# Top-64 attention on one NeuronCore: the copy of turned probabilities lags its item by one turn more

## What is computed

```python
scores = jnp.einsum('bhqd,bhkd->bhqk', qh, kh) / np.sqrt(DHEAD)
vals, idx = jax.lax.top_k(scores, topk)          # topk = 64 of 77 keys
scores = jnp.full_like(scores, neg).at[bI, hI, qI, idx].set(vals)
probs = jax.nn.softmax(scores, axis=-1)
ctx = jnp.einsum('bhqk,bhkd->bhqd', probs, vh)
return ctx.transpose(0, 2, 1, 3).reshape(...) @ wo_w.T + wo_b
```

## Time and profile before

| | us |
|---|---|
| median of 3 runs | 897.32 |
| lowest, highest | 896.64, 900.05 |
| the profiled execution | 897.16 |
| its span | 895.4 |
| PE busy | 801.0 (89%) |
| VectorE busy | 655.2 (73%) |
| ScalarE busy | 497.2 (56%) |
| GpSimd busy | 531.4 (59%) |
| mean granted TensorE clock | 0.968 |

### The profile page before, as it was taken

The page is one execution under the profiler, slowest core; times in us unless marked ns, Lnnn a source line. Parts: engine busy times, 40 slices in busy tenths (PEclk is TensorE's granted clock), DMA queues, the critical chain, the costliest instruction groups (busy, mean ns, idle before and its releaser), DMA issues.

```text
span 895.4 us, 18961 instructions
## 1 busy us (share of the span) xinstructions
PE 801.0 (89%) x5858; PEld 628.7 (70%) x5858; DVE 655.2 (73%) x2739; ACT 497.2 (56%) x1287; POOL 531.4 (59%) x721
## 2 busy tenths in 40 slices
PE   6999998998788676867887989999999999998897
PEld 5677775886566444645666779788778879987775
DVE  4888686888979999999999873455455542516887
ACT  5778764568997797978877331222112122226673
POOL 3565644676752978878775125456455545237883
PEclk9999999999999697979999899999999999999999
DMA  9200001000000082000222621222222243140011
GB/s 296 62 1 2 2 1 48 1 1 1 1 1 1 2 328 97 1 25 2 71 72 87 227 72 36 37 42 43 37 42 43 36 87 58 19 107 1 13 36 48
DMA packets 37823, 46.70 MB, mean 52 GB/s; under 512 B 4327, under 2 KB 33871, under 8 KB 37724
## 3 DMA queue, kind: packets, MB, share of 16 engines
q1 hardware_dynamic: 29243, 35.77, 11.9%
q0 software_dynamic: 8480, 9.72, 7.1%
HBM read 33.80 MB, written 11.68 MB: 51 GB/s over the span
## 4 chain that ended last, share of the span: by engine, by line
PE 64%; DVE 14%; ACT 8%; issue 6%; POOL 6%; another core or an unknown queue 1%; DMA 1%; DVEq 0%; ACTq 0%; POOLq 0%; SPq 0%
PE ps L3012 10%; PE ps L3023 10%; PE ps L2358 4%; PE ps L2454 3%; PE ps L2481 3%; PE ps L2780 3%; PE ps L2800 3%; PE ps L3067 2%; PE ps L3041 2%; PE ps L2439 2%; ACT ptall L1254 2%; PE ps L2466 2%; DVE experts L1812 1%; PE ps L2811 1%; PE ps L2866 1%
## 5 line engine op out<-in xcount | busy, mean ns | idle before, releaser
L2080 DVE COPY ptall<-experts 128x512 f32 x136 | 53.3, 434 | 97.8 <-PE ps L3012 49.1
L1388 ACT ACTIVATE wk<-ps 128x1024 f32<-128x1024 f32 x34 | 34.9, 1025 | 131.3 <-PE ps L3012 69.1
L3012 PE MATMUL ps<-xnT,ptall 128*128 128x128 f32 x896 | 105.0, 275 | 2.3 <-DVE ptall L2080 1.8
L3012 PEld LDWEIGHTS ps<-xnT,ptall 128*128 128x128 f32 x896 | 102.4, 192 | 3.0 <-issue 3.0
L3023 PE MATMUL ps<-experts,wk 128*128 x448 | 102.0, 381 | 1.4 <-ACT xkeep L1398 1.4
L3023 PEld LDWEIGHTS ps<-experts,wk 128*128 128x128 f32 x448 | 82.9, 190 | 17.0 <-issue 6.8
L848 POOL DMA_INDIRECT xn<-expert_in,rown x34 | 36.0, 1058 | 80.7 <-PE ps L2998 57.1
L646 POOL TENSOR_TENSOR experts<-experts,rden 128x616 f32<-128x616 f32 x32 | 38.9, 1217 | 46.8 <-DVE rden L1572 46.8
L872 POOL DMA_INDIRECT token_sum<-xkeep,dest x28 | 47.6, 1699 | 31.1 <-ACT xkeep L1398 22.5
L1229 ACT ACTIVATE experts<-experts 128x77 f32<-128x77 f32 x248 | 62.1, 258 | 0.0
L2358 PE MATMUL ps<-ones 128*128 128x256 bf16 x434 | 55.7, 286 | 5.8 <-POOL mone L599 5.8
(11 more groups left out here) (382 smaller groups left out, 2358.5 us busy)
## 6 DMA issues: line engine op xcount, KB each, us to landing
experts<-in_ew SPq DMA_DIRECT2D x16, 1024.0 KB, 8.5
xkeep<-in_bw SPq DMA_DIRECT2D x2, 1024.0 KB, 7.3
expert_in<-xkeep SPq DMA_DIRECT2D x8, 256.0 KB, 3.9
x<-token_sum SPq DMA_DIRECT2D x8, 256.0 KB, 3.8
out<-x SPq DMA_DIRECT2D x7, 256.0 KB, 2.2
x<-in_x SPq DMA_DIRECT2D x1, 1536.0 KB, 9.1
token_sum<-x SPq DMA_DIRECT2D x4, 256.0 KB, 2.6
token_sum<-x SPq DMA_DIRECT2D x1, 1024.0 KB, 4.5
```

The costliest lines, as they stand in the source:

```text
L2080: ins = nc.vector.tensor_copy(tilew[:, v, c, :], experts[:, bass.ds(e * EW + (c * FF + v * 512), 512)])
L3012: ins = nc.tensor.matmul(ps[j % 2][:, v, k * P:(k + 1) * P], tilew[:, v, c, k * P:(k + 1) * P], xTb[j % 3][:, c, :], start=c == 0, stop=c ...
```

## The change

On ScalarE the copy of turned probabilities of turn k is now that of item k-3 instead of k-2, and stands behind the absolute values and the scores and ahead of the exponentials; from turn 31 on it catches up (items 28 and 29 in one turn). The output copy moves from ahead of the scores to behind the exponentials. On PE the values of item k-3 stand at the head of turn k, behind the scores; the turning of x and the queries come one turn later (turns 4, 12, 20 and 5, 6, 13, 14, 21, 22) and ahead of the transposes of the same turn. The warming matmuls are left out where the turn has a part of the output projection. A wait for the copy of routing rows moves into top_values. No work is added.

```diff
@@ scalar, turn k @@
-                    if k >= 3 and (k - 3) // 2 % 2:
+                    if k >= N4 and (k - 3) // 2 % 2:
                         top_out(k - 3)
...
                     if 1 <= k < N4 - 1:
                         top_scores(k + 1)
+                    if 3 <= k < N4:
+                        top_turned_probs(k - 3)
                     if 1 <= k < N4:
                         top_exp(k - 1, 0)
...
+                    if 3 <= k < N4 and (k - 3) // 2 % 2:
+                        top_out(k - 3)
                     if k in top_parts:
                         top_residual(top_parts[k] // 4, top_parts[k] % 4, k)
-                    if 2 <= k < N4 + 2:
+                    if N4 - 1 <= k < N4 + 2:
                         top_turned_probs(k - 2)
@@ tensor, top_probs and top_values @@
-                    q, j = (i + 1) // ITEMS + 1, (i + 1) % ITEMS
+                    q, j = (i + 2) // ITEMS + 1, (i + 2) % ITEMS
                     pe.wait_ge(pt_s[4].sem, pt_s[4].past(i))
-                    if N4 - 9 <= i < N4 - 1:
+                    if N4 - 9 <= i < N4 - 1 and i + 2 not in top_parts:
                         warm(14, 4)
                     pe.wait_ge(nm_s, i + 1)
-                    if q < PAIRS and j == 3:
+                    if q < PAIRS and j == 4:
                         pe.wait_ge(xts[4].sem, xts[4].past(2 * q + 2))
-                    elif q < PAIRS and j in (4, 5):
-                        pe.wait_ge(q_s[4].sem, q_s[4].past(4 * q + 2 * (j - 3)))
+                    elif q < PAIRS and j in (5, 6):
+                        pe.wait_ge(q_s[4].sem, q_s[4].past(4 * q + 2 * (j - 4)))
...
+                    if i - 1 in l5_at:
+                        pe.wait_ge(xts[5].sem, xts[5].past(l5_at[i - 1] + 1))
@@ tensor, turn k @@
+                    if 3 <= k < N4:
+                        top_values(k - 3)
                     if k in top_parts:
                         top_final(top_parts[k] // 4, top_parts[k] % 4, k)
+                    if q + 1 < PAIRS:
+                        if j == 4:
+                            top_turn(q + 1)
+                        if j in (5, 6):
+                            top_queries(q + 1, j - 5)
                     if 2 <= k < N4 + 2:
                         top_probs(k - 2)
                         if k - 2 in l5_at:
                             l5_flip_half(l5_at[k - 2], k)
-                        if k - 3 in l5_at:
-                            pe.wait_ge(xts[5].sem, xts[5].past(l5_at[k - 3] + 1))
...
-                        top_values(k - 2)
+                        if k >= N4 - 1:
+                            top_values(k - 2)
...
-                    if q + 1 < PAIRS:
-                        if j == 3:
-                            top_turn(q + 1)
-                        if j in (4, 5):
-                            top_queries(q + 1, j - 4)
```

## The result

| | before | changed |
|---|---|---|
| median, us (20 runs of each) | 900.83 | 902.11 |
| lowest to highest | 895.31 to 903.31 | 899.15 to 909.43 |
| ratio, 95% interval | | 1.0036 (1.0019 to 1.0054) |
| span of the profiled execution | 895.4 | 900.1 |
| stretch from VectorE's first item to the start of the last values | 222.80 | 226.32 |

The changed kernel is slower by 0.36%, some 3.2 us (the means of the two differ by 3.0 us, the medians by 1.3). Forecast were 897.0 with a range of 893 to 902, and a kernel 0.4 us faster than before. The interval of the ratio leaves out 1, but the change is smaller than the 0.5% that the prediction's chances counted. The stretch runs from the first reduction of the top-64 items (at 273.67 and 275.71 us) to the start of the last values (496.47 and 502.03). It grew by 3.5 us, which is about the size of the whole loss.

The account below looks back on a forecast made before the run. VectorE was taken to bound the top-64 stage at 6.36 us an item, with 3.8 us of idle time to give back. From 897.16 us, -3.8 + 3.4 gave 896.8, stated as 897.0, range 893.0 to 902.0.

Parts of the forecast that it names:

- The old waits go: Top-64 stage: ScalarE's 20.2 us wait for turned probabilities goes, with VectorE's idle at items 12, 19, 20, 31; gain 3.8 us.
- Paces: ScalarE in the top-64 stage: its other work costs the same, a plain turn 4.2 us of 6.36.
- The new waits: Query copies, pairs 1 to 3: waits of 1.9 us, 3.3 in turns 14 and 22; 0.6 us idle at item 16.
- The clock, and pair 3: TensorE's half-clock windows stay; new VectorE idle 1.0, 1.2, 1.2 us in pairs 1 to 3, sum 3.4.
- Warming matmuls: Items 24 to 27 lose their 14 on TensorE; nothing comes back, range nothing to 2 us lost.
- The end: From turn 31 on the lag is caught up; taken as 0, with 0 to 1.1 us gained.
- clock falls in the query turns: Half clock in turns 12 to 14 or 20 to 22 lengthens waits: 904.8 us, last turn alone 900.6; chance 0.16.
- clean gain: ScalarE's query waits are hidden, new idle time 0, end gives 1.1 us: 892.3 us, 893.4 without the end; chance 0.15.
- No effect: VectorE's idle places come back because GpSimd's hold causes them, not the copy: 897.2 us; chance 0.05.
- GpSimd's hold: At turns 8 and 16 GpSimd stands for ScalarE's squares, 1.51 us; pair 3 starts 1.3 us late from it.

## Why the prediction was wrong

By its steps:

1. *The old waits go*: right in the main. The 20.2 us on flipped probabilities are gone, and so are the idle places at items 12 and 31. The 3.8 us were one execution's; a second had 3.0. Item 19 kept 0.18 us of 0.92, but item 20 did not go (0.87 for 0.65). Its turn 18, with the projection in a half-clock window, took 7.33 us; where the projection ran at full clock (the version with the warming matmuls back) it took 6.01 and item 20 had no idle time.
2. *Paces*: right in the main. Turns 13 and 14 came out within 0.03 us, though in turn 13 the query wait was shorter than worked out and ScalarE's other pieces 0.2 us longer, and turn 12 took 6.2 us for 6.4.
3. *The new waits*: right in number and place. Singly they are 1.66 and 3.00 us at full clock, not 1.9 and 3.3: the 0.3 us to drain was too much, for ScalarE's copy starts 0.03 us behind the last query matmul. That the sum is 14.2 again (14.4 in the second profile) is luck, as the wait of turn 21 at half clock makes up for it; with that turn at full clock it was 12.6. For pair 2 the 0.97 us at item 16 lie in the 0.6 to 1.2 that was summed, but the second profile had 1.66, and with turn 12 at half clock it was 2.8.
4. *The clock, and pair 3*: **this failed.** The sum gave pair 3 1.2 us; it took 4.0 (1.69 and 2.29), and 4.1 in the second profile. I kept the half-clock windows where the old order had them, while the lagged order has its own: in every profile of it but the one with the added matmuls a stretch of 6.8 us or more at half clock began between 411 and 421 us; in the five of the old order there was none there or one of 3.4. So turn 21, summed at full clock with 8.1 us, took 9.7, and turn 20, summed with 6.0, took 7.1; turn 22 was 8.7 as forecast. At full clock turn 21 took 8.13 us in the version with the added matmuls. The routing logits and flips ahead of its values, which the sum left out, cost nothing there; they count at half clock alone. The three turns took 25.6 us where 22.8 was summed, and the idle time is 2.8 us over the sum as well. Of these 2.8 the clock makes some 2.5 (1.6 in turn 21, and 0.9 in turn 20, an estimate from the added matmuls). The rest is the wait of the absolute values for the flips of turn 20, which the sum does not have. The range of pairs 2 and 3, 0.6 to 3 us each, did not reach it. Pair 1, given 1.0, took none and, in the second profile, some 0.6. The argument had also read the old clock too kindly: besides the three stretches it names, the kernel before has two of 3.4 us, from 358.2 (in turn 12) and from 443.6, so not all the query turns had run at 1.00.
5. *Warming matmuls*: their loss caused nothing that could be shown.
6. *The end*: no change beyond what two profiles of one kernel differ by (14.5 and 16.2 before, 15.6 and 14.8 after).

New idle time was 6.0 and 7.4 us instead of 3.4. Less the old 3.8 and 3.0, that is 2.2 and 4.4 us more; the end adds 1.0 in the first pair of profiles and gives back 1.3 in the second, and small gaps make up the 3.5 us by which the stretch grew in each. The rival *clock falls in the query turns* named the mechanism, and was given 0.16, because those turns had run at 1.00 in the old order. Its 900.6 is near what came, but by luck: it priced the last turn of a pair, at 3.9 us, and that turn (22) ran at full clock, while turns 20 and 21, priced at 1.5 and 2.6, ran partly at half. The rival *clean gain* is refuted by the six waits. *No effect* has the half of it that GpSimd's hold did cause the idle places of the old order at items 12 and 19. The absolute time was 5.1 us above the forecast, and 3.5 of that has another reason: the kernel before has a median of 900.8 over 20 runs, not the 897.3 of the three shown. Against the kernel before, the forecast was 0.4 us faster, and 3.2 us slower (by the ratio) came.

What stays open is what in the lagged order makes the clock fall in pair 3; the split between query waits and clock rests on the one profile with added matmuls. In the changed kernel TensorE's single waits for ScalarE's copy are longer (up to 4.2 us, 2.7 before; the lists of waits of TensorE from 289 to 480 us of the changed kernel and from 290 to 495 of the one before):

```profile
PE ps L2817 <- ACT ptall L1254: 35.3, 21, 4.2
```

```profile
PE ps L2811 <- ACT ptall L1254: 30.6, 26, 2.7
```

The longest do not stand ahead of the window at 417.4: there TensorE had stood 1.97 us ahead of the values of turn 20 and 0.83 us for the copy of turned x. With the added matmuls these were 1.38 and 0.83 us, and no window followed. Whether the shorter stand or the added work kept the clock up was not tested alone. The Trainium skill's page "TensorE: Matmul & The Clock Gate", section "HAM oscillation — how this bites in real kernels", describes a loop of short matmul bursts parted by waits for DMA, in which each burst starts cold again. The waits here are for ScalarE's copies, and the two profiles agree with it in kind.

## What to carry to other kernels

A lag that takes one wait out of a ring of two engines brings another in wherever a second user of the same buffer is squeezed into the same turn: write out the ring, turn by turn, for those turns alone, with everything TensorE does in them. Sum the granted clock as a result of the new order, not as a row of the old one, and let the range hold two more turns partly at half clock. Check a sum of waits one by one: here 14.2 us agreed while none of the six did. Where two profiles of one kernel differ by 2 us, an idle place of 1 us is a lead and not a finding.

## What the runs showed of the hardware

Fewer matmuls made the stretch no shorter: with half of the query matmuls it was 227.7 us (226.3 and 227.0 with all), the half clock lasted 20.5 us instead of 6.8, and the query waits fell by 0.9 us, where 5.8 was worked out. With 14 warming matmuls cut to 5 ahead of five flips the end was 18.0 us, against 14.5 and 16.2. With eight matmuls added to turn 21, and no half clock in it, the turn was 1.6 us shorter (8.13 for 9.71 us).
